# The first gated dense layer: its weights split in the last heads of the first attention, side products between the turnings, four output banks

## What is computed

```python
x = x + _L0_xattn_ref(_layernorm(x), ctx_4096, mask, position_bias, ln_weight, w_q, w_k, w_v, w_out)  # 32 heads of 128
x = x + _L0_ffn_ref(_layernorm(x), W_base, b_base, W_router, b_router, lora_A, lora_B)

def _L0_ffn_ref(x, W_base, b_base, W_router, b_router, lora_A, lora_B):
    base_out = jnp.einsum('bsd,od->bso', x, W_base) + b_base
    logits = jnp.einsum('bsd,ed->bse', x, W_router) + b_router      # 8 experts
    weights = sparsemax(logits)
    h = jnp.einsum('bsd,edr->bser', x, lora_A)                      # rank 16 each
    expert_out = jnp.einsum('bser,bse,ero->bso', h, weights, lora_B)
    return base_out + expert_out
```

## Time and profile before

| | us |
|---|---|
| three runs | 3024.07, 3029.74, 3027.27 (median 3027.27) |
| the profiled execution, its own time | 3025.75 |
| its span, first to last instruction | 3023.6 |
| the first attention, up to PE's last matmul in it | 0 to 879.2 |
| the gated layer, between its two barriers | 881.7 to 958.7 |
| granted TensorE clock, mean over the span | 0.971 |

### The profile page before, as it was taken

One profiled execution on the slowest core, in us unless ns is written; L12 is line 12 of the kernel. 1 busy time (PEld: TensorE's weight loads), 2 busy tenths in 40 slices (PEclk: granted clock), 3 DMA queues, 4 the chain that ended last, 5 costly groups with the idle time before them and its releaser, 6 DMA issues. The chain is left out here.

```text
span 3023.6 us, 44597 instructions
## 1 busy us (share of the span) xinstructions
PE 2829.5 (94%) x16196; PEld 2451.1 (81%) x16196; DVE 2007.0 (66%) x3531; ACT 1429.4 (47%) x3473; POOL 1326.2 (44%) x1180
## 2 busy tenths in 40 slices
PE   7999999999986996999999999988999999999977
PEld 6888888888874884778888877868999899898865
DVE  5787778877765778789999974344454444545453
ACT  3666656566631673144454433215545545455530
POOL 6455545545421754565555530013434434444430
PEclk9999999999987997999999999999999999999988
DMA  3121212212121002111111103100001000000000
GB/s 131 52 67 55 59 56 66 66 48 63 44 84 44 15 5 70 39 43 43 42 43 43 33 21 123 42 22 22 29 18 29 29 19 29 26 28 22 18 29 28
DMA packets 77816, 131.85 MB, mean 44 GB/s; under 512 B 10016, under 2 KB 23584, under 8 KB 77216
## 3 DMA queue, kind: packets, MB, share of 16 engines
q1 hardware_dynamic: 68096, 112.09, 12.3%
q10 hardware_dynamic: 9504, 16.91, 1.7%
HBM read 114.23 MB, written 14.75 MB: 43 GB/s over the span
## 5 line engine op out<-in xcount | busy, mean ns | idle before, releaser
L89 PE MATMUL a_pa<-a_wo,a_ot 128*128 128x512 f32 x2304 | 536.6, 391 | 13.0 <-issue 9.3
L89 PEld LDWEIGHTS a_pa<-a_wo,a_ot 128*128 128x128 f32 x2304 | 430.0, 188 | 106.9 <-issue 18.4
L356 DVE SCALAR_TENSOR_TENSOR a_nf_acc<-a_nf_t,a_nf_acc 128x512 f32<-128x512 bf16 (+1 forms) x462 | 401.9, 870 | 35.2 <-ACT a_nf_t L309 4.9
L89 PE MATMUL a_pa<-h_t,a_wqk 128*128 128x512 f32 x1536 | 372.6, 395 | 1.7 <-DVE h_t L769 1.7
L309 ACT ACTIVATE a_nf_t<-a_nf_w,a_nf_shifts 128x512 bf16<-128x512 f32 (+1 forms) x495 | 321.1, 709 | 59.0 <-DVE a_nf_acc L356 33.7
L89 PEld LDWEIGHTS a_pa<-h_t,a_wqk 128*128 128x128 f32 x1536 | 281.8, 188 | 55.8 <-DVE h_t L769 1.9
L89 PE MATMUL a_pa<-a_wv,ctx_t 128*128 128x512 f32 x960 | 232.3, 398 | 30.7 <-POOL a_wv L526 16.7
L89 PEld LDWEIGHTS a_pa<-a_wv,ctx_t 128*128 128x128 f32 x960 | 180.3, 191 | 68.0 <-issue 16.7
L89 PE MATMUL a_pa<-ctx_t,a_wqk 128*128 128x512 f32 x960 | 224.8, 390 | 2.5 <-POOL a_wqk L1679 2.2
L1010 POOL TENSOR_TENSOR a_prob<-a_prob,a_inv 128x512 f32<-128x512 f32 x128 | 132.5, 1057 | 210.8 <-DVE a_inv L1391 210.8
L89 PEld LDWEIGHTS a_pa<-ctx_t,a_wqk 128*128 128x128 f32 x960 | 179.7, 188 | 41.3 <-POOL a_wqk L1679 4.2
(11 more groups left out here) (363 smaller groups left out, 6114.2 us busy)
## 6 DMA issues: line engine op xcount, KB each, us to landing
a_raw<-in_a_w SPq DMA_DIRECT2D x288, 256.0 KB, 2.6
a_nf_w<-in_nf ACTq DMA_DIRECT2D x32, 256.0 KB, 2.7
nf_rounded<-a_nf_acc ACTq DMA_DIRECT2D x32, 256.0 KB, 2.0
f_rows<-nf_rounded SPq DMA_DIRECT2D x22, 256.0 KB, 3.1
ctx_kept<-ctx_t SPq DMA_DIRECT2D x1, 4096.0 KB, 16.5
ctx_t<-ctx_kept SPq DMA_DIRECT2D x1, 4096.0 KB, 15.0
f_cols<-nf_rounded SPq DMA_DIRECT2D x11, 256.0 KB, 3.9
a_ctx_raw<-in_ctxt SPq DMA_DIRECT2D x4, 512.0 KB, 7.6
```

Source lines behind the costliest of these rows:

```text
L89: ins = nc.tensor.matmul(out, lhs(a), rhs(b), start=first and i == 0, stop=last and i == 2)
L356: ins = nc.vector.scalar_tensor_tensor(acc, t, c, acc, inner, outer)
```

## The change

In the attention: the two weight matrices of the gated layer are loaded by SP after all of the attention's weights, into space that the attention no longer uses by then, and POOL splits them: the side weights behind head 28's splits, two quarters of the base weights behind `make_bias` of head 29's turn, the other two behind the `norm_weights` of head 30's turn (and so ahead of `split(("o", 31))`).

In the gated layer: PE turns blocks 0 to 3, then alternates one turning (4 to 7) with one block of side products (0 to 3), then does the side products of 4 to 7; each block's side products wait for that block's LO alone. DVE takes the logits of a block between the steps of the norm. The base products have four banks: blocks 0, 1 and 2 come before the wait for the gates, then both groups of turnings of `low`, then block 3, then the expert parts of 0 to 3, and from block 4 on base and expert part by turns. On DVE the bias additions to `x` now stand behind the splits of the turned `low` (four behind each), and one small operation of the sparsemax is merged with the next. POOL in this stage splits only the small `lora_b`.

```diff
+    def start_on_vector(self, dve): ...            # TransposedNorm.on_vector taken apart: start_on_vector, applied, low
+    def transposes(self, pe, b): ...
@@ bias_attention_stage, SP
+            sp.wait_ge(a_ready, made_count["v", QUADS - 1, NB - 1])
+            sp.dma_start(f0["raw_side"][:, :, :], side_in.rearrange("(c p) n -> p c n", p=P)).then_inc(side_loaded, 16)
+            sp.dma_start(f0["raw"][:, :, :], base_in.rearrange("(c p) n -> p c n", p=P)).then_inc(base_loaded, 16)
@@ POOL
+            def prefetch_side():
+                pool.wait_ge(a_ready, made_count["v", QUADS - 1, NB - 1])
+                pool.wait_ge(side_loaded, 16)
+                nc.gpsimd.tensor_scalar(f0["side"][:, HI, :, :], f0["raw_side"][:, :, :], 1.0, 0.0, ALU.mult, ALU.add
+                                        ).then_inc(side_hi, 1)
+                pool.wait_ge(side_hi, 1)
+                nc.gpsimd.tensor_tensor(f0["side"][:, LO, :, :], f0["raw_side"][:, :, :], f0["side"][:, HI, :, :].bitcast(F32),
+                                        ALU.subtract).then_inc(low_done, 1)
+            def prefetch_base(c):
+                if c == 0:
+                    pool.wait_ge(o_ready, 2 * (H - 4))
+                    pool.wait_ge(base_loaded, 16)
+                nc.gpsimd.tensor_scalar(f0["base"][:, HI, c, :], f0["raw"][:, c, :], 1.0, 0.0, ALU.mult, ALU.add
+                                        ).then_inc(base_hi, 1)
+                pool.wait_ge(base_hi, c + 1)
+                nc.gpsimd.tensor_tensor(f0["base"][:, LO, c, :], f0["raw"][:, c, :], f0["base"][:, HI, c, :].bitcast(F32),
+                                        ALU.subtract).then_inc(low_done, 1)
@@ for h in range(H): at the end of each head
+                if h == H - 4:
+                    prefetch_side()
+                elif h == H - 3:
+                    prefetch_base(0)
+                    prefetch_base(1)
+                elif h == H - 2:
+                    prefetch_base(2)
+                    prefetch_base(3)
@@ ffn0_stage, SP
-            sp.dma_start(raw_side[:, :, :], side_in.rearrange("(c p) n -> p c n", p=P)).then_inc(loaded_side, 16)
-            sp.dma_start(raw[:, :, :], base_in.rearrange("(c p) n -> p c n", p=P)).then_inc(loaded, 16)
@@ POOL
-            nc.gpsimd.tensor_scalar(base[:, HI, :, :], raw[:, :, :], 1.0, 0.0, ALU.mult, ALU.add).then_inc(base_split, 1)
-            nc.gpsimd.tensor_tensor(base[:, LO, :, :], raw[:, :, :], base[:, HI, :, :].bitcast(F32),
-                                    ALU.subtract).then_inc(base_split, 1)
@@ PE
-            norm.on_tensor(pe)
-            pe.wait_ge(side_split, 1)
-            for b in range(NB): ...
+            for b in range(4):
+                norm.transposes(pe, b)
+            for b in range(4, NB):
+                norm.transposes(pe, b)
+                side_products(b - 4)
+            for b in range(4, NB):
+                side_products(b)
+            for b in range(3):
+                base_products(b)
+            pe.wait_ge(gate_ready, 1)
+            turned(0)
+            turned(1)
+            base_products(3)
+            pe.wait_ge(lora_split, 2)
             for b in range(NB):
-                if b >= 2:
-                    pe.wait_ge(out_used, b - 1)
-...
+                if b >= 4:
+                    base_products(b)
+                lora_products(b)
@@ side_products(b): before its matmuls
+                pe.wait_ge(norm.lo_done, b + 1)
                 if b >= 2:
                     pe.wait_ge(side_used, b - 1)
@@ base_products(b): before its matmuls
+                if b >= 4:
+                    pe.wait_ge(out_used, b - 3)
@@ DVE
-            steps.mark(nc.vector.tensor_copy(side[:, HI, :, :], raw_side[:, :, :]))
+            norm.start_on_vector(dve)
+            for b in range(1, NB):
+                norm.applied(dve, b)
+                if b >= 3:
+                    norm.low(dve, b - 3)
+                if b >= 5:
+                    logits(b - 5)
+            for b in range(NB - 3, NB):
+                norm.low(dve, b)
+                logits(b - 2)
+            logits(NB - 2)
+            logits(NB - 1)
-            for b in range(NB):
-                steps.mark(nc.vector.tensor_tensor(x[:, b, :], x[:, b, :], b_base[:, :], ALU.add))
             for t in range(2):
                 dve.wait_ge(tr_hi, t + 1)
                 nc.vector.tensor_tensor(dst, p_tr[:, t, :], hi.bitcast(F32), ALU.subtract).then_inc(tr_lo, 1)
+                for b in range(4 * t, 4 * t + 4):
+                    steps.mark(nc.vector.tensor_tensor(x[:, b, :], x[:, b, :], b_base[:, :], ALU.add))
```

More of the change, by code:

```diff
@@ L2136, in rope_attention_stage, with ffn0_prefetch, at @@
     st.close()
-E0, R0 = 8, 16
-def ffn0_stage(nc, x, ident, h_t, base_in, side_in, lora_b_in, b_base_in, b_router_in, ctx_t, ctx_kept, carried, ahead):
+def ffn0_prefetch(nc, st, free_at):
+    KB = 1024
+    SIDE = E0 * R0 + E0
+    def at(offset, name, shape, dt=F32):
+        return nc.alloc_sbuf_tensor_at(f"f0_{name}", shape, dt, offset=free_at + offset)
+    w = dict(base=at(0, "base", [P, 2, DC, D], F32R), raw=at(48 * KB, "raw", [P, DC, D]),
+             raw_side=at(56 * KB, "raw_side", [P, DC, SIDE]), side=at(56 * KB + 4 * DC * SIDE, "side", [P, 2, DC, SIDE], F32R))
+    sems = {n: st.sem("f0_" + n) for n in ("side_loaded", "base_loaded", "side_hi", "base_hi", "low_done")}
+    return w, sems
@@ L2167, in ffn0_stage @@
-    (loaded, loaded_side, side_split, base_split, side_ready, side_used, own, gate_ready, tr_ready, tr_hi, tr_lo,
-     out_ready, out_used, ranked, ctx_stored) = (st.sem(n) for n in (
-         "loaded", "loaded_side", "side_split", "base_split", "side_ready", "side_used", "own", "gate_ready",
-         "tr_ready", "tr_hi", "tr_lo", "out_ready", "out_used", "ranked", "ctx_stored"))
-    norm = TransposedNorm(nc, st, carried, x, ident, h_t, [t[:, n, :] for t in (p_side, p_tr) for n in range(2)],
-                          st.sb("norm_h", [P, NB, D]))
+    base, side = weights["base"], weights["side"]
@@ new lines, in at, with small @@
+    def at(offset, name, shape, dt=F32):
+        return nc.alloc_sbuf_tensor_at(f"f0_{name}", shape, dt, offset=free_at + offset)
+    raw_b = at(16 * KB, "raw_b", [P, D])
+    lora_b = at(18 * KB, "lora_b", [P, 2, D], F32R)
+    b_base = at(22 * KB, "b_base", [P, D])
+    low = at(24 * KB, "low", [P, NB, E0 * R0])
+    place = [28 * KB]
+    def small(name, shape):
+        place[0] += int(np.prod(shape[1:])) * 4
+        return at(place[0] - int(np.prod(shape[1:])) * 4, name, shape)
+    b_router = small("b_router", [P, E0])
@@ L2174, in ffn0_stage @@
+    norm = TransposedNorm(nc, st, carried, x, ident, h_t, [p_out[:, n, :] for n in range(4)],
+                          at(64 * KB, "norm_h", [P, NB, D]))
     with nc.Block() as block:
@@ L2239, in _, with logits @@
         def _(dve):
-            norm.on_vector(dve)
             steps = Steps(dve, own)
-            dve.wait_ge(loaded_side, 32)
-            steps.mark(nc.vector.tensor_copy(side[:, HI, :, :], raw_side[:, :, :]))
-            steps.wait()
-            nc.vector.tensor_tensor(side[:, LO, :, :], raw_side[:, :, :], side[:, HI, :, :].bitcast(F32),
-                                    ALU.subtract).then_inc(side_split, 1)
-            for b in range(NB):
+            def logits(b):
+                if b == 0:
+                    dve.wait_ge(loaded_side, 16)
                 dve.wait_ge(side_ready, b + 1)
```

159 lines of the change are left out of this document (81 added, 78 removed).

## The result

The kernel before took 3026.03 us (median of 4), the changed one 3003.16 us (median of 4: 2999.27, 3000.03, 3006.28 and 3012.34). The ratio is 0.9925, with a 95% interval of 0.9911 to 0.994. The predicted time was 3004.0, in a range of 2999 to 3017. Size and sign agree.

What follows compares the result with a forecast made beforehand. PE, busy 94% of the span, bounds the kernel through waits and lower clock. Layer -26.2, POOL's split +2.0, clock in the gap +1.2, DVE +0.3: -22.7 us, 3003.1 or by the median 3004.6, said 3004; range 2999 to 3017.

Steps and rivals of the forecast that it cites:

- The rival: Gated layer: side products stay at the lower clock, total change -10.7 us, 3015 by the profiled execution; chance 0.18.
- wrong if the level at 888 to 900 is the lower one: Sign in the changed profile: side products at the lower clock from 888 to 900 would refute the prediction.
- the clock came back by 888.0: Gated layer: upper clock from 888.0, so 92 side products take 10.9 us and end at 900.2, 14.8 us less.
- the forecast case: Side products at the upper clock; the layer 26.2 us less, in all -22.7 us, 3004 us; chance 0.70.
- my first rival: Same as The rival: side products at the lower clock, 3015, by the median 3016.6; chance 0.18.
- Price of a side product: Gated layer: one 136-column matmul at the upper clock costs 119 ns, bounds 119 and 123.
- POOL's quarters ahead of `split(("o", 31))`: Attention's end: base quarters 2 and 3 delay POOL's split, so PE starts the last output products 2.0 us later.
- Clock falling in the new gap: Ahead of the attention's last output products: PE's longer idle time may lower the clock, +1.2 us, bounds 0 and 1.8.
- DVE beside POOL: Attention's last heads: DVE's rounding steps slow while POOL splits quarters 0 and 1, +0.3 us, bounds 0 and 1.5.
- Side split and quarters 0 and 1: Attention's last heads: these POOL splits, 2.7 and 4 to 5.2 us, fit POOL's idle time and cost POOL nothing.
- rival 4: Side part: DVE becomes the later one, PE waits 0.5 us a block: 3008; chance 0.08 shared with another rival.
- 2 and 3: POOL's pieces slow DVE's rounding: 3009 (0.08 with rival 4); clock falls before the last output products and stays low: 3044 (0.02).

Runs made afterwards that it cites:

- e1: Changed kernel plus unread filler matmuls in PE's gaps: 8 behind the attention's last output, 3 ahead of and 5 behind the first turning; median 2999.34 us, ratio 0.9907.
- e0: The changed kernel again, unaltered, six executions from 2997.37 to 3016.07 us; median 3008.66 us, ratio 0.9928 against the kernel before.
- e4: e1 with the eight bias additions put ahead of the splits of the turned `low` on DVE; median 2997.67 us, ratio 0.9902.
- e5: e1 with only base product 0, instead of three products, ahead of the wait for the gates; median 3002.6 us, ratio 0.9922.
- e7: e1 with the edits of e2 and e4 added; median 2995.42 us, ratio 0.9898.
- e11: The same kernel as e7, run another time; median 2998.62 us, ratio 0.9908.
- e8: Kernel before, without the change, plus fillers: 8, 3 and 5 as in e1, 16 behind the last turning; median 3025.09 us of ten, ratio 0.9992.
- e9: e1 and e3 together: fillers (reading the context), side and base weights loaded and split in the gated layer; median 3007.77 us, ratio 0.993.
- e3: Changed kernel with loads and splits of side and base weights back in the gated layer, on SP and POOL; median 2999.07 us, ratio 0.9907.
- e2: Changed kernel with base quarters 2 and 3 split behind head 31's output weights instead of ahead; median 2995.16 us, ratio 0.9904.
- e10: Changed kernel with the edits of e2 and e4, no fillers; median 2998.02 us of six, ratio 0.9916.
- e6: e1 with all eight turnings ahead of the side products and DVE's logits behind the whole norm; median 3003.3 us, ratio 0.9921.

## Why the prediction was right and where it was wrong

**Right: both cases as mechanisms, and their sums within the layer.** For the lower clock I had 20.7 us of side products and -4.6 and -9.6 for the two parts of the layer; the profile gave -4.8 and -9.6. For the upper clock I had the side products ending at 900.2, then 30.2 us to the last matmul with a stall of 1.8 in it and gates 2.2 us ahead of PE. Measured in e1: 900.0, 30.4, 1.73; DVE's gating step ended at 905.69 and PE came to it at 908.14, 2.4 ahead. The rival's total by the profiled execution was 3015, measured 3012.3; the forecast's total is taken apart below.

**Wrong: the weighing of the two.** By its own sign ("wrong if the level at 888 to 900 is the lower one") the prediction failed in both profiled executions. The step that failed is "In the trace the clock came back by 888.0 ... I take that". It carried a chance of 0.70 to 0.18, and a single number. By times and mean clocks, the forecast case came in four of ten executions and the rival in six; only two of the ten have a profile, and both are the rival. The predicted 3004.0 lies where no execution of this kernel lay. The median of 3003.16 hit it by luck: it is the middle of two on either side, and six more executions (e0) had their median at 3008.66. I had read one instant of one execution (a rise at 888.0 under the turnings) as a property of the kernel. In the kernel before that rise did no good either: the clock fell again at 891.4, ahead of the side products of the earlier trace rows.

**Why one level or the other.** Shown: the same side products can run at either level from their first to their last. They ran 23 us at 0.50 with PE busy throughout, and 12 us at 1.00. Not shown, but in line with the profiles: what stands directly ahead matters. With gaps filled and no wait ahead of them (e1, e4, e5, e7, e11) the level was 1.00 in five profiles of five; behind a wait of 1.06 or 1.68 us the clock fell in them (e8, e9). Such a wait does not decide alone: by their times two of ten executions of e8 and two of four of e9 escaped the fall, and in e3, where the clock had just risen, a wait of 0.76 us did not bring it down. Not settled: what decides in the changed kernel as it is. In the five profiles of kernels with the new order and without fillers, this is how it went: fell 883.8 and 884.2, 0.5 and 0.6 us after the first turning's start (the changed kernel, e0), and stayed low; fell 885.0, 882.9 and 886.3 (e3, e2, e10), 1.0 to 2.1 us after it, and was up again by 888.4, 886.3 and 889.7. Where it stayed low, PE's idle 1.0 us behind the first turning lay wholly inside the low stretch. That fits as a cause; five profiles don't show it, and I made no run that shifts it alone.

The rise in e10 (889.7) came when PE had done nothing but turnings since 882.0, and that in e3 (888.4) likewise. In the changed kernel's two profiles the turnings, and 96 side products behind them, did not raise the clock. The Trainium skill (TensorE: Matmul & The Clock Gate, Part 4) says that a matmul in transpose mode, which a turning is, "doesn't count as PE-busy the same way" and that the upper level does not engage for it. The two rises are against this, as the earlier trace rows were; the other two profiles are in line with it. I had set the rule aside for what one trace showed; its result, my first rival, came more often than not.

**Mis-sized, in the sum** (each against the rows of the forecast case):
- *Price of a side product*: 119 ns taken from 64 columns, 112 measured. 0.6 us for 92 of them, mine too high.
- *POOL's quarters ahead of `split(("o", 31))`, +2.0*: the wait is there and released by POOL, as named. But POOL's split ended at 868.91, and DVE's last `ot` at 868.60: 0.3 us on the path in this profile, and the comparison under e2 says the same. The cover that I had measured (2.07) had grown, because the clock fell at 863.4 and head 31's values' product took 3.31 us. Where that fall isn't, the two quarters (863.08 to 866.95, 3.9) less the cover would still cost 1.8; no profile shows that case.
- *Clock falling in the new gap, +1.2*: nothing. The last 48 output products took 11.17 us, in e2 with the old gap 11.12. The fall came before, and also in e3 and e8, where no split was moved there; in the profile of before it wasn't there. So it is not this order's. I had priced a fall behind the gap and not seen that the place ahead of it could fall as well.
- *DVE beside POOL, +0.3*: the eight rounding steps went from 7.85 to 10.09 us, as expected, and PE's waits of heads 28 to 31 are no longer for it: nothing.
- *Side split and quarters 0 and 1*: nothing, as said; POOL was idle for 5.5 and 11.8 us behind them.
- The four together are 0.6+1.7+1.2+0.3 = 3.8 us too much: 3004-3.8 = 3000.2 for the forecast case. The four executions that by times and clocks are this case have 2997.4 to 3000.0; what the rest is, no profile of them shows.

**The other rivals.** PE never waited for DVE between the groups of side products (groups with a turning start 1.75 us apart in e1, less than my 1.85), so rival 4 did not come; neither did 2 and 3.

**Where the gain lies.** In e1, the forecast case with fillers, the next stage begins 26.4 us sooner (932.4 instead of 958.8), although the first turning begins 1.6 us later. From the first turning on, the side products begin 3.9 instead of 12.1 us later, -8.2: they need neither the whole norm nor a late split on DVE. In e6, which has the changed waits and splits and the fillers but no interleaving, they begin 7.0 us behind the first turning, so 5.0 of the 8.2 come from waits and splits and 3.2 from the interleaving. From there to the first base product it is 12.0 instead of 20.5 us, -8.5, with three turnings now inside: that is the clock, and in the changed kernel's own profile this part took 22.8, +2.3. From the first base product to the last matmul it is -11.2 (in the changed kernel's profile -9.6). Between e1's profile and the changed kernel's lie 12.9 us, nearly all of it because the clock did not return. Up to the first base product the interleaving is worth 1.9 (e6), and splitting the weights in the attention instead of on POOL in the layer 1.0 to 1.3 without fillers (e3) and 1.9 with them (e9). The larger part of the 5.0 us therefore lies in taking the split off DVE and waiting block by block, not in the move into the attention.

## What to carry to other kernels

A long run of narrow matmuls can stay at the lower clock from end to end (23 us here), so see that PE goes into it at the upper level. Fillers where PE would idle anyway did this here (e1, e4, e7, e11: 16 executions of 16 without the slow case), but not, by their times, in eight of ten executions of e8 and two of four of e9, where a wait stayed directly ahead of the run. When a sum hangs on a clock level at one instant of one profile, look at several executions (their mean granted clocks are enough) before weighing it, and give two numbers if the level can be either. A product placed ahead of a wait is worth its cover, and also what the wait would do to the clock behind it (e5: 2.9 us of wait, and 3.0 us more for the clock).

## What the runs showed of the hardware

- One kernel, unaltered, has two times about 12 us apart in 3000: 2997 to 3000 us with a mean granted clock of 0.976 to 0.978, 3006 to 3016 us with 0.971 to 0.974 (four and six executions). Both profiles of the upper group have one group of matmuls at the lower level; that the lower group has it at the upper level is inferred from its times and from e1, e2, e3 and e10.
- 136-column matmuls, back to back: 214 ns each at 0.50, 112 ns at 1.00. At 0.50 they kept PE busy for 12.00 of 12.00 us and the clock did not rise; it rose at 914.6, when the 512-column products begun at 911.18 were running (in e0 at 914.9, begun at 911.33).
- In e8 and e9 the clock was up when such products began (895.34, 892.43) and fell with PE busy on them (897.5, 893.9); just before them PE had been idle for 1.06 and 1.68 us. Through four idle times of 0.38 to 0.40 us between turnings (e6) it held.
